# Turning and writing the gate weights of two pairs of images at once, in a MetaFormer block with a mixture of experts

## The chip, the cores and the metric

The kernel runs on one core of a Trainium2 chip. The metric is the device time of one execution in microseconds. The core has TensorE (PE, matmuls; PEld is its weight load), VectorE (DVE), ScalarE (ACT), GpSimd (POOL) and SyncE (SP), which here issues the transfers.

## What is computed

The input has 8 images of 64 channels and 16 x 16 pixels. After a layer norm over channels comes a convolutional linear attention, added to the input. The pixels are then tokens of 64 channels, and each passes a layer norm, a gate and eight experts:

```python
gate_logits = xf @ Wg + bg
top_w, top_i = jax.lax.top_k(gate_logits, TOP_K)          # TOP_K = 2
top_w = jax.nn.softmax(top_w, axis=-1)
w_dense = jnp.sum(jax.nn.one_hot(top_i, E, dtype=xf.dtype) * top_w[..., None], axis=1)
for e in range(E):                                        # E = 8
    h = jax.nn.gelu(xf @ W1[e] + b1[e], approximate=False)
    out = out + w_dense[:, e:e + 1] * (h @ W2[e] + b2[e])
x = from_tokens(t + out, x)
```

All is float32. `w_dense` (8 weights for each token, two of them not zero) is what the change is about.

## The kernel before

The eight images are worked on as four pairs, s = 0 to 3. A pair has 512 tokens: four tiles of 128, two for each image. All eight experts are computed for all tokens, and the result of each is multiplied by its gate weight.

**The gate.** VectorE works out the gate weights for two pairs together, a part (`softmax(0)` for pairs 0 and 1, `softmax(1)` for pairs 2 and 3). L808 writes them into `WDN`, where tokens lie on partitions. It runs at 66 us for part 0 and at 81 us for part 1.

**From there to where they are used.** An expert's result lies the other way, channels on partitions and tokens along the row. So the weights must be turned, and each row of them must stand on 64 partitions. This is done for each pair by itself: in `tokens(s)` TensorE makes two transposes of gate weights (L1079, one for each half of an image's tokens) into PSUM and then two transposes of the pair's tokens (L1082). In `read_tokens(s)` ScalarE copies the turned weights into `WT` (L509, 16 rows of 256) and the tokens into `outs`, which is `XP` in the profile (L510). SyncE, in `spread_weights(s)`, writes `WT` to memory (`spread_dram`, L308), waits for it to land, and then loads it back with every row repeated on 64 partitions into `WB` (L315; `WB` is part of `BAND` in the profile). `WB` has two slots, s % 2. From pair 2 on the loads also wait until the slot has been read.

**The experts.** `first_layer(s, e)` makes the hidden values of an expert (matmuls at L911, four of 512 columns), ScalarE applies gelu (L518), `second_layer(s, e)` (L1123) makes the result, recorded as eight matmuls of 256 columns. `combine(s, ep)` on VectorE takes two experts: `weigh` (L826) adds the bias and multiplies by `WB`, giving `WY`, and `add_up` (L832) adds it to `outs`. For the last pair GpSimd does seven of the eight additions (L396). `store(s)` (L322) writes a pair's result.

**The order** is written out by hand on each engine. On TensorE, around the change: `second_layer(0, 0..3)`, `tokens(0)`, `xt(3)` (four transposes, L1052), `first_layer(0, 7)`, `first_layer(1, 0..3)` with `gate(1)` in it, `second_layer(0, 4..7)`, `tokens(1)`, `first_layer(1, 4..7)`, `second_layer(1, 0..3)`, `tokens(2)`, `first_layer(2, 0..3)`, `second_layer(1, 4..7)`, `first_layer(2, 4..7)`, `second_layer(2, 0..3)`, `tokens(3)`, `first_layer(3, 0..3)`, `second_layer(2, 4..7)`, `first_layer(3, 4..7)`, `second_layer(3, 0..7)`. A result's place in PSUM is taken again once `y_read` says that VectorE has weighed what was there: `second_layer(0, 6)` waits for experts 0 and 1 of pair 0, `second_layer(1, 2)` for experts 4 and 5.

On SyncE, after the inputs: `spread_weights(0)`, `spread_weights(1)`, `store(0)`, `spread_weights(2)`, `store(1)`, `spread_weights(3)`, `store(2)`, `store(3)`.

Of the kernel before, what the change touches and what calls it, by code (L numbers as in the profile page):

```python
# [21 lines left out]
ALU = mybir.AluOpType  # L22
ACT = mybir.ActivationFunctionType
# [3 lines left out]
N = H * W  # L27
# [8 lines left out]
NW = HD + HEADS  # L36
E, HID, KC = 8, 256, 2
PAIRS = B // 2
TILES = 4
PT = TILES * 128  # L40
LN_C_EPS, LN_T_EPS, BN_EPS, ATT_EPS = 1e-6, 1e-5, 1e-5, 1e-15
# [28 lines left out]
def build(nc, x, w_qkv, w_dw, w_pw, w_proj, vectors, wg, w1, b1, w2, b2, consts, select, out):  # L70
    ctx = ExitStack()
    with ctx:  # L72
        def sb(name, shape, dt=F32):
            return ctx.enter_context(nc.sbuf_tensor(name, shape, dt))

        def sem(name):
            return ctx.enter_context(nc.semaphore(name))
# [4 lines left out]
        IDT = sb("IDT", [128, 128])  # L82
# [22 lines left out]
        SEL = sb("SEL", [LOW + DX * I, SELW], F32R)  # L105
        WD = sb("WD", [LOW + DX * I, G * DY], F32R)
        WGS = sb("WGS", [128, 2, E], F32R)
        WT = sb("WT", [2 * E, 2, N])
        W1H, W1L = sb("W1H", [128, E * HID], F32R), sb("W1L", [128, E * HID], F32R)
        RS = sb("RS", [128, G, DY, W])  # L110
        BAND = sb("BAND", [128, G * DY * 128])
# [11 lines left out]
        XBM = sb("XBM", [128, 16])  # L123
        SQ2 = sb("SQ2", [128, 2, TILES, C + 1])
        KR = sb("KR", [128, PAIRS, 4, HD])
        VM = sb("VM", [128, PAIRS, 2, 4, 2, KW])
        KV = sb("KV", [128, 2, 2, NW])
        DEN = sb("DEN", [128, 2, TILES, HEADS])
        SM = sb("SM", [128, PAIRS, 2, TILES])
        XS = sb("XS", [128, PAIRS, PT], F32R)  # L130
        PLACE = sb("PLACE", [128, 16, E], mybir.dt.uint32)
        GAP = sb("GAP", [128, 5, 16])
        WDN = sb("WDN", [128, PAIRS, 2, 2, E])

        band = BAND[:, :].rearrange("p (g d m) -> p g d m", g=G, d=DY)

# [4 lines left out]
        def late(*dims):  # L141
            first = taken[0]
            taken[0] += int(np.prod(dims))
            assert taken[0] <= G * DY * 128
            names = " ".join("abcde"[:len(dims)])
            return BAND[:, first:taken[0]].rearrange(f"p ({names}) -> p {names}", **dict(zip("abcde", dims)))
# [3 lines left out]
        QT = late(2, 2, N)  # L150
        ATT = late(2, TILES, HD)
        ATTT = late(2, PT)
        X2 = late(8, 2, C)
        XC2 = late(2, TILES, C)
        XHL = late(2, TILES, 2, C)
# [11 lines left out]

        outs = XP[:, :].rearrange("p (s n) -> p s n", s=PAIRS)

        PAR = CST[:, C_PAR:C_PAR + 2]  # L170

        PS = ctx.enter_context(nc.psum_tensor("PS", [128, 8, 512], F32))
        PARTS = 2
        OF_PART = PAIRS // PARTS
        SOFTMAX_PARTS = slice(0, OF_PART * TILES), slice(OF_PART * TILES, PAIRS * TILES)

        STATS_BANKS, WQC_BANK, WARM_BANK = (0, 1, 6, 2), 7, 7
# [11 lines left out]
        TOKEN_BANK = 5  # L189
# [35 lines left out]
        gap_ready, exp_ready, wdn_ready = sem("gap_ready"), sem("exp_ready"), sem("wdn_ready")  # L225
        turned, wt_read, tokens_read, wt_out = sem("turned"), sem("wt_read"), sem("tokens_read"), sem("wt_out")
# [55 lines left out]
        spread = nc.dram_tensor("spread_dram", (PAIRS, 2 * E, N), F32, kind="Internal").ap()  # L282
# [3 lines left out]
        @block.sync  # L286
        def _(sp):
            sp.dma_start(X[:, 0:2 * N], x[:, 0:2 * N]).then_inc(x_in[0], 16)
            sp.dma_start(X[:, 2 * N:4 * N], x[:, 2 * N:4 * N]).then_inc(x_in[1], 16)
            for h in range(2):  # L290
                sp.dma_start(WQ[C * h:C * h + C, :], w_qkv).then_inc(wq_in, 16)
            sp.dma_start(PW[:, :, :].rearrange("p g o -> p (g o)"),
                         w_pw.unsqueeze(0).broadcast_to([W, I, QKV])).then_inc(pw_in, 16)
            sp.dma_start(CST[:, :], consts).then_inc(cst_in, 16)
            sp.dma_start(VEC[:, :], vectors.unsqueeze(0).broadcast_to([128, 4 * C + E])).then_inc(vec_in, 16)
            sp.dma_start(WP[:, :], w_proj).then_inc(wp_in, 16)
            for h in range(2):
                sp.dma_start(WG[C * h:C * h + C, :], wg).then_inc(w1_in, 16)
                sp.dma_start(W1[C * h:C * h + C, :].rearrange("c (e n) -> c e n", e=E),
                             w1.rearrange("e c n -> c e n")).then_inc(w1_in, 16)  # L300
            sp.dma_start(W2[:, :, :].rearrange("p k c -> p (k c)"), w2).then_inc(w2_in, 16)
            sp.dma_start(B1[:, :], b1).then_inc(b1_in, 16)
            for h in range(2):
                sp.dma_start(B2[C * h:C * h + C, :], b2).then_inc(b2_in, 16)

            def spread_weights(s):
                sp.wait_ge(wt_read, s + 1)
                sp.dma_start(spread[s], WT[:, s % 2, :]).then_inc(wt_out, 16)  # L308
                sp.wait_ge(wt_out, 16 * (s + 1))
                if s >= 2:  # L310
                    sp.wait_ge(y_read, E * (s - 1))
                parts = ((0, 1), (1, 2), (2, 4)) if s == 0 else ((0, 2), (2, 4))
                for first, last in parts:
                    for b in range(2):
                        i = sp.dma_start(WB[C * b:C * b + C, s % 2, 2 * first:2 * last, :],  # L315
                                         spread[s, E * b + 2 * first:E * b + 2 * last, :].unsqueeze(0)
                                         .broadcast_to([C, 2 * (last - first), N]))
                        i.then_inc(wb_in[s % 2][first], 16)

            def store(s):  # L320
                sp.wait_ge(out_ready, s + 1)
                sp.dma_start(out[2 * s:2 * s + 2].rearrange("b c y x -> (b c) (y x)"), outs[:, s, :]).then_inc(stored, 16)  # L322

            spread_weights(0)
            spread_weights(1)
            store(0)
            spread_weights(2)
            store(1)
            spread_weights(3)
            store(2)  # L330
            store(3)
            sp.wait_ge(stored, 16 * PAIRS)
# [66 lines left out]
        def _(act):  # L399
# [104 lines left out]
            def read_tokens(s):  # L504

                act.wait_ge(turned, s + 1)
                if s >= 2:
                    act.wait_ge(wt_out, 16 * (s - 1))
                act.activation(WT[:, s % 2, :], PS[0:2 * E, TOKEN_BANK, N:2 * N], ACT.Copy).then_inc(wt_read, 1)  # L509
                act.activation(outs[:, s, :], PS[:, TOKEN_BANK, 0:N], ACT.Copy).then_inc(tokens_read, 1)  # L510

            def gelu(s, e):
# [56 lines left out]
        def _(dve):  # L569
# [223 lines left out]
            def softmax(part):  # L793
                tiles, pairs = SOFTMAX_PARTS[part], slice(OF_PART * part, OF_PART * (part + 1))
                O1, O2 = ONEHOT[:, 0, tiles], ONEHOT[:, 1, tiles]
                ex, dn, q1, q2 = (GAP[:, k, tiles] for k in (1, 2, 3, 4))

                def wide(v):
                    return v.unsqueeze(2).broadcast_to([128, tiles.stop - tiles.start, E])

                dve.wait_ge(exp_ready, part + 1)
                link(dve.tensor_scalar(dn, ex, 1.0, None, ALU.add))
                link(dve.reciprocal(q1, dn))
                link(dve.tensor_tensor(q2, ex, q1, ALU.mult))
                dve.tensor_tensor(O1, O1, wide(q1), ALU.mult)
                link(dve.tensor_tensor(O2, O2, wide(q2), ALU.mult))
                for b in range(2):
                    dve.tensor_tensor(WDN[:, pairs, :, b, :], O1.rearrange("p (s b h) e -> p b s h e", b=2, h=2)[:, b],  # L808
                                      O2.rearrange("p (s b h) e -> p b s h e", b=2, h=2)[:, b], ALU.add)\
                        .then_inc(wdn_ready, 1)  # L810

            def combine(s, ep):
# [96 lines left out]
        def _(pe):  # L909
# [146 lines left out]
            def gate(part):  # L1056

                pairs = range(OF_PART * part, OF_PART * (part + 1))
                for s in pairs:
# [11 lines left out]
            def tokens(s):  # L1071

                if s == 0:
                    pe.wait_ge(b_read[PAIRS - 1], B_PROJ)
                else:
                    pe.wait_ge(tokens_read, s)
                pe.wait_ge(wdn_ready, 2 * (s // OF_PART) + 2)
                for half in range(2):
                    pe.transpose(PS[0:2 * E, TOKEN_BANK, N + 128 * half:N + 128 * half + 128],  # L1079
                                 WDN[:, s, half].rearrange("p b e -> p (b e)"), IDT[:, :])  # L1080
                for half in range(2):
                    i = pe.transpose(PS[:, TOKEN_BANK, 128 * half:128 * half + 128],  # L1082
                                     X2[:, 2 * s + half].rearrange("p b c -> p (b c)"), IDT[:, :])
                i.then_inc(turned, 1)
# [147 lines left out]
```

## Time and profile before

| | |
|---|---|
| time, median of 3 runs | 127.3 us (127.17 to 127.38) |
| the profiled execution | 127.27 us, span 125.6 us |
| PE busy | 120.7 us (96%) |
| PEld busy | 98.1 us (78%) |
| VectorE busy | 85.9 us (68%) |
| ScalarE busy | 84.6 us (67%) |
| GpSimd busy | 28.7 us (23%) |
| granted TensorE clock | 1.000 |
| chain that ended last | PE 89%, DVE 3%, ACT 2% |

The span is from the first to the last instruction of the one execution that was profiled. The time has the start and the end of the execution besides. In rows of the trace, a line begins with the start in us from the beginning of the span and the time in us; "x16" is the number of instructions merged in the line, and what stands in brackets is the idle time of the engine before it and what ended it. Matmuls overlap, so several can be shown as running at the same time.

### The profile page before, as it was taken

What the parts mean: (1) busy time and instruction counts of PE and PEld (TensorE: products, weight loads), DVE (VectorE), ACT (ScalarE), POOL (GpSimd) and SP (SyncE); (2) the same over time, 40 slices, a digit from 0 to 9 for tenths busy, and PEclk for the clock granted to TensorE, in tenths of its full rate; (3) what the DMA queues carried; (4) which work ended last, traced back from release to release, by engine and by line L of the source; (5) the groups of instructions that cost most, each with busy time, mean ns of one, the idle gap of its engine ahead of it and who ended that gap; (6) DMA issues with size and microseconds to landing.
All of it is one profiled execution on the core that took longest, in us unless ns stands there. A gap on an engine that the chain in (4) does not pass through costs nothing.

```text
span 125.6 us, 2675 instructions
## 1 busy us (share of the span) xinstructions
PE 120.7 (96%) x916; PEld 98.1 (78%) x916; DVE 85.9 (68%) x273; ACT 84.6 (67%) x199; POOL 28.7 (23%) x35
## 2 busy tenths in 40 slices
PE   6999999999999999999999999999999999999990
PEld 6998899999999889897786786665866668666650
DVE  0789999999987887997985049991809155081552
ACT  4369999999973948159795597393782928739100
POOL 7007999600000000303280004000000000000681
PEclk9999999999999999999999999999999999999999
DMA  3789300000000000000000027039375100841001
GB/s 94 223 180 240 111 3 0 3 5 0 0 0 0 5 0 0 0 5 0 0 0 3 10 104 224 7 87 215 87 205 134 42 0 5 227 115 42 0 0 42
DMA packets 5078, 7.59 MB, mean 60 GB/s; under 512 B 1442, under 2 KB 3530, under 8 KB 5066
## 3 DMA queue, kind: packets, MB, share of 16 engines
q1 hardware_dynamic: 4832, 7.28, 22.0%
q10 hardware_dynamic: 234, 0.15, 0.4%
q8 instruction: 7, 0.11, 0.4%
q14 instruction: 5, 0.04, 0.1%
HBM read 6.84 MB, written 0.59 MB: 59 GB/s over the span
## 4 chain that ended last, share of the span: by engine, by line
PE 89%; DVE 3%; ACT 2%; issue 1%; POOL 1%; POOLq 1%; DVEq 0%
PE PS L911 57%; PE PS L1123 21%; PE PS L1015 3%; DVE MS L623 2%; PE PS L1021 2%; PE PS L927 1%; PE PS L1052 1%; POOL XP L396 1%; PE PS L1038 1%; PE PS L1079 1%; PE PS L975 1%; ACT RS L418 1%; PE PS L1082 1%; POOLq L72 1%; ACT MS L518 1%
## 5 line engine op out<-in xcount | busy, mean ns | idle before, releaser
L518 ACT ACTIVATE MS<-PS,B 128x512 f32<-128x512 f32 x48 | 28.9, 679 | 7.0 <-PE PS L911 7.0
L826 DVE SCALAR_TENSOR_TENSOR WY<-PS,B,BAND 128x256 f32<-128x256 f32 x32 | 14.4, 480 | 21.1 <-PE PS L1123 17.7
L911 PE MATMUL PS<-QP,BAND 128*128 128x120 f32 (+2 forms) x240 | 27.0, 275 | 0.2 <-DVE QP L646 0.2
L911 PEld LDWEIGHTS PS<-QP,BAND 128*128 128x128 f32 x240 | 26.9, 192 | 0.4 <-issue 0.4
L911 PE MATMUL PS<-XS,W1H 128*128 128x512 f32 x64 | 26.5, 414 | 0.0
L911 PE MATMUL PS<-XS,W1L 128*128 128x512 f32 x64 | 25.3, 396 | 0.0
L1123 PE MATMUL PS<-MS,W 128*64 128x256 f32 x192 | 22.3, 383 | 0.0
L1123 PEld LDWEIGHTS PS<-MS,W 128*64 128x64 f32 x192 | 13.2, 137 | 8.5 <-ACT MS L518 1.5
L436 ACT ACTIVATE BAND<-RS,PW 128x80 f32<-128x80 f32 x64 | 17.2, 429 | 0.0
L911 PEld LDWEIGHTS PS<-XS,W1H 128*128 128x128 f32 x64 | 12.0, 188 | 4.8 <-issue 0.9
L396 POOL TENSOR_TENSOR XP<-XP,WY 128x256 f32<-128x256 f32 x7 | 5.1, 727 | 41.1 <-DVE WY L826 40.2
L911 PEld LDWEIGHTS PS<-XS,W1L 128*128 128x128 f32 x64 | 12.1, 189 | 1.8
L376 POOL TENSOR_TENSOR SM<-SM,HALF 128x4 f32<-128x4 f32 x4 | 4.0, 1007 | 33.6 <-DVE SM L743 33.6
L832 DVE TENSOR_TENSOR XP<-XP,WY 128x256 f32<-128x256 f32 x25 | 10.5, 420 | 0.6 <-POOL XP L396 0.2
L579 DVE TENSOR_TENSOR BAND<-RS,PW 128x640 f32<-128x640 f32 x14 | 10.8, 807 | 0.0
L518 ACT ACTIVATE BAND<-PS,B 128x512 f32<-128x512 f32 x16 | 9.8, 698 | 0.0
L509 ACT ACTIVATE WT<-PS 16x256 f32<-16x256 f32 x4 | 1.5, 374 | 11.0 <-PE PS L1082 11.0
L1123 PE MATMUL PS<-BAND,W 128*64 128x256 f32 x64 | 7.6, 379 | 0.0
L1123 PEld LDWEIGHTS PS<-BAND,W 128*64 128x64 f32 x64 | 4.6, 137 | 2.3
L381 POOL TENSOR_TENSOR GAP<-EULER,GAP 128x8 f32<-128x8 f32 x2 | 3.3, 1636 | 12.0 <-DVE GAP L779 12.0
L649 DVE STREAM_TRANSPOSE QP<-MS 128x384 f32<-128x384 f32 x7 | 6.0, 858 | 0.0
L492 ACT ACTIVATE BAND<-PS 128x512 f32<-128x512 f32 x4 | 2.4, 597 | 4.9 <-PE PS L1038 4.9
(120 smaller groups left out, 168.6 us busy)
## 6 DMA issues: line engine op xcount, KB each, us to landing
BAND<-spread_dram SPq DMA_DIRECT2D x14, 256.0 KB, 4.6
W<-in_w_dram SPq DMA_DIRECT2D x3, 512.0 KB, 6.1
X<-in_x_dram SPq DMA_DIRECT2D x2, 256.0 KB, 3.2
BAND<-spread_dram SPq DMA_DIRECT2D x4, 128.0 KB, 2.9
out_dram<-XP SPq DMA_DIRECT2D x4, 128.0 KB, 1.7
VEC<-in_vectors_dram SPq DMA_DIRECT2D x1, 132.0 KB, 3.0
SELF<-in_select_dram ACTq DMA_DIRECT2D x1, 100.8 KB
WQ<-in_w_qkv_dram SPq DMA_DIRECT2D x2, 48.0 KB, 3.4
```

The source lines that it names most:

```text
L376: pool.tensor_tensor(SM[:, s, 1, :], SM[:, s, 0, :], HALF[:, 0:TILES], ALU.pow).then_inc(r2_ready, 1)
L381: pool.tensor_tensor(GAP[:, 1, tiles], EULER[:, tiles], GAP[:, 0, tiles], ALU.pow).then_inc(exp_ready, 1)
L396: pool.tensor_tensor(outs[:, s, :], outs[:, s, :], WY[:, e % 2, :], ALU.add).then_inc(added, 1)
L436: i = act.activation(band[:, g].rearrange("p d (x o) -> p o (d x)", o=I)[:, o], RS[:, g].rearrange("p d x -> p (d x)"), ACT.Copy, scale=PW ...
L518: act.activation(hidden(n), PS[:, h_bank(n), :], ACT.Gelu, bias=B1[:, k:k + 1]).then_inc(gelu_done, 1)
L579: dve.tensor_tensor(*band_factors(g), ALU.mult).then_inc(band_v, 1)
L649: dve.transpose(qp[:, 3 * h:3 * h + 3], head(h)).then_inc(qp_ready, 1)
L826: dve.scalar_tensor_tensor(out=WY[:, e % 2, :], in0=PS[:, bank, at:end], scalar=B2[:, e:e + 1], in1=WB[:, s % 2, e, :], op0=ALU.add, op1=A ...
L832: i = dve.tensor_tensor(outs[:, s, :], outs[:, s, :], WY[:, e % 2, :], ALU.add)
L911: return pe.matmul(PS[0:parts, bank, cols[0]:cols[1]], lhsT, rhs, start=start, stop=stop)
L1015: i = pe.matmul(PS[rows, CHAIN_BANK[s], 0:2 * KW], KR[:, s, r, rows], VM[:, s, half, r].rearrange("p b v -> p (b v)"), start=r == 0, stop= ...
L1123: i = pe.matmul(PS[C * b:C * b + C, bank, at:end], W2[:, KC * e + k, :], hidden(KC * (E * s + e) + k)[:, N * b:N * b + N], start=k == 0, s ...
```

## The change

The gate weights of a part, two pairs, are turned and written together. `WDN` is laid out anew, so that for one half of the tokens the 32 values of two pairs (2 pairs, 2 images, 8 experts) stand side by side. `tokens(s)` turns gate weights only for s = 0 and s = 2, with two transposes that give 32 rows, and waits for the gate only there. `read_tokens(s)` copies `WT` only there too, now 32 rows of 256. SyncE writes both pairs' weights in one transfer (`write_weights`), for part 0 ahead of `spread_weights(0)` and for part 1 ahead of `spread_weights(2)`. The loads themselves are as before, as are the transposes and copies of the tokens. The diff, but for the moved constants (`PARTS = 2`, `OF_PART = PAIRS // PARTS`):

```diff
@@ -105,7 +107,7 @@
         SEL = sb("SEL", [LOW + DX * I, SELW], F32R)
         WD = sb("WD", [LOW + DX * I, G * DY], F32R)
         WGS = sb("WGS", [128, 2, E], F32R)
-        WT = sb("WT", [2 * E, 2, N])
+        WT = sb("WT", [2 * OF_PART * E, PARTS, N])
         W1H, W1L = sb("W1H", [128, E * HID], F32R), sb("W1L", [128, E * HID], F32R)
         RS = sb("RS", [128, G, DY, W])
         BAND = sb("BAND", [128, G * DY * 128])
@@ -130,7 +132,7 @@
         XS = sb("XS", [128, PAIRS, PT], F32R)
         PLACE = sb("PLACE", [128, 16, E], mybir.dt.uint32)
         GAP = sb("GAP", [128, 5, 16])
-        WDN = sb("WDN", [128, PAIRS, 2, 2, E])
+        WDN = sb("WDN", [128, 2, PAIRS, 2, E])
 
         band = BAND[:, :].rearrange("p (g d m) -> p g d m", g=G, d=DY)
 
@@ -303,10 +303,13 @@
             for h in range(2):
                 sp.dma_start(B2[C * h:C * h + C, :], b2).then_inc(b2_in, 16)
 
+            def write_weights(part):
+                sp.wait_ge(wt_read, part + 1)
+                sp.dma_start(spread[OF_PART * part:OF_PART * (part + 1)].rearrange("s r n -> (s r) n"),
+                             WT[:, part, :]).then_inc(wt_out, 16)
+                sp.wait_ge(wt_out, 16 * (part + 1))
+
             def spread_weights(s):
-                sp.wait_ge(wt_read, s + 1)
-                sp.dma_start(spread[s], WT[:, s % 2, :]).then_inc(wt_out, 16)
-                sp.wait_ge(wt_out, 16 * (s + 1))
                 if s >= 2:
                     sp.wait_ge(y_read, E * (s - 1))
                 parts = ((0, 1), (1, 2), (2, 4)) if s == 0 else ((0, 2), (2, 4))
@@ -321,9 +324,11 @@
                 sp.wait_ge(out_ready, s + 1)
                 sp.dma_start(out[2 * s:2 * s + 2].rearrange("b c y x -> (b c) (y x)"), outs[:, s, :]).then_inc(stored, 16)
 
+            write_weights(0)
             spread_weights(0)
             spread_weights(1)
             store(0)
+            write_weights(1)
             spread_weights(2)
             store(1)
             spread_weights(3)
@@ -504,9 +509,9 @@
             def read_tokens(s):
 
                 act.wait_ge(turned, s + 1)
-                if s >= 2:
-                    act.wait_ge(wt_out, 16 * (s - 1))
-                act.activation(WT[:, s % 2, :], PS[0:2 * E, TOKEN_BANK, N:2 * N], ACT.Copy).then_inc(wt_read, 1)
+                if s % OF_PART == 0:
+                    act.activation(WT[:, s // OF_PART, :], PS[0:2 * OF_PART * E, TOKEN_BANK, N:2 * N], ACT.Copy)\
+                        .then_inc(wt_read, 1)
                 act.activation(outs[:, s, :], PS[:, TOKEN_BANK, 0:N], ACT.Copy).then_inc(tokens_read, 1)
 
             def gelu(s, e):
@@ -805,8 +810,8 @@
                 dve.tensor_tensor(O1, O1, wide(q1), ALU.mult)
                 link(dve.tensor_tensor(O2, O2, wide(q2), ALU.mult))
                 for b in range(2):
-                    dve.tensor_tensor(WDN[:, pairs, :, b, :], O1.rearrange("p (s b h) e -> p b s h e", b=2, h=2)[:, b],
-                                      O2.rearrange("p (s b h) e -> p b s h e", b=2, h=2)[:, b], ALU.add)\
+                    dve.tensor_tensor(WDN[:, :, pairs, b, :], O1.rearrange("p (s b h) e -> p b h s e", b=2, h=2)[:, b],
+                                      O2.rearrange("p (s b h) e -> p b h s e", b=2, h=2)[:, b], ALU.add)\
                         .then_inc(wdn_ready, 1)
 
             def combine(s, ep):
@@ -1074,10 +1079,11 @@
                     pe.wait_ge(b_read[PAIRS - 1], B_PROJ)
                 else:
                     pe.wait_ge(tokens_read, s)
-                pe.wait_ge(wdn_ready, 2 * (s // OF_PART) + 2)
-                for half in range(2):
-                    pe.transpose(PS[0:2 * E, TOKEN_BANK, N + 128 * half:N + 128 * half + 128],
-                                 WDN[:, s, half].rearrange("p b e -> p (b e)"), IDT[:, :])
+                if s % OF_PART == 0:
+                    pe.wait_ge(wdn_ready, 2 * (s // OF_PART) + 2)
+                    for half in range(2):
+                        pe.transpose(PS[0:2 * OF_PART * E, TOKEN_BANK, N + 128 * half:N + 128 * half + 128],
+                                     WDN[:, half, s:s + OF_PART].rearrange("p s b e -> p (s b e)"), IDT[:, :])
                 for half in range(2):
                     i = pe.transpose(PS[:, TOKEN_BANK, 128 * half:128 * half + 128],
                                      X2[:, 2 * s + half].rearrange("p b c -> p (b c)"), IDT[:, :])
```

## Rows read from the trace of the kernel before

**Rows 1.** One stretch: busy us of PE, PEld, DVE, ACT, POOL; PEclk, DMA share, GB/s.

```profile
41.00:119.00 78.00, 77.94 (x560) 57.61 (x556) 48.19 (x187) 51.83 (x99) 8.98 (x9) 1.00 0.23 61
```

**Rows 2.** The chain that ended last, in time: start, us, what.

```profile
76.47 3.60 PE PS L1123 x32
...
84.36 3.60 PE PS L1123 x32
87.96 0.32 PE PS L1079 x2
...
88.50 3.74 PE PS L911 x16
...
95.84 3.93 PE PS L911 x16
```

**Rows 3.** Timeline at `tokens(2)`: start, us, engine, line.

```profile
87.89 0.10 PEld L1079 LDWEIGHTS PS<-IDT,WDN 128*16 128x16 f32 x2 [0.39 <-issue]
87.89 0.39 PE L1079 MATMUL PS<-IDT,WDN 128*16 128x128 f32 x2
88.01 0.25 PEld L1082 LDWEIGHTS PS<-IDT,BAND 128*128 128x128 f32 x2
...
88.57 0.39 PE L911 MATMUL PS<-XS,W1L 128*128 128x512 f32 x1
```

**Rows 4.** Timeline, a changeover without `tokens`.

```profile
95.77 0.19 PEld L911 LDWEIGHTS PS<-XS,W1H 128*128 128x128 f32 x1 [0.38 <-issue]
...
96.11 0.40 PE L911 MATMUL PS<-XS,W1L 128*128 128x512 f32 x1
```

**Rows 5.** Timeline at `tokens(0)` and `xt(3)`, eight transposes.

```profile
69.86 0.39 PE L1079 MATMUL PS<-IDT,WDN 128*16 128x128 f32 x2
...
70.31 0.60 PE L1052 MATMUL PS<-IDT,BAND 128*128 128x128 f32 x4
...
70.98 0.39 PE L911 MATMUL PS<-XS,W1L 128*128 128x512 f32 x1
```

**Rows 6.** Groups of weight loads: busy us, mean ns, idle before.

```profile
L1082 PEld LDWEIGHTS PS<-IDT,BAND 128*128 128x128 f32 x8 | 1.0, 140 | 0.1
...
L1079 PEld LDWEIGHTS PS<-IDT,WDN 128*16 128x16 f32 x8 | 0.4, 89 | 1.5 <-issue 1.5
```

**Rows 7.** Timeline of ScalarE at `read_tokens(1)`.

```profile
80.65 0.37 ACT L509 ACTIVATE WT<-PS 16x256 f32<-16x256 f32 x1 [2.90 <-PE PS L1082]
80.93 0.36 ACT L510 ACTIVATE XP<-PS 128x256 f32<-128x256 f32 x1
```

**Rows 8.** Issues of transfers: count, KB each, median us to landing.

```profile
BAND<-spread_dram SPq DMA_DIRECT2D x14, 256.0 KB, 4.6
...
BAND<-spread_dram SPq DMA_DIRECT2D x4, 128.0 KB, 2.9
...
spread_dram<-WT SPq DMA_DIRECT2D x4, 16.0 KB, 1.4
```

**Rows 9.** Timeline of SyncE's queue: the time is that of the issues.

```profile
72.37 3.65 SPq L315 DMA_DIRECT2D BAND<-spread_dram  x6
...
82.47 2.37 SPq L315 DMA_DIRECT2D BAND<-spread_dram  x4
```

**Rows 10.** Timeline of VectorE's weighing, pairs 0 and 1.

```profile
76.57 0.88 DVE L826 SCALAR_TENSOR_TENSOR WY<-PS,B,BAND 128x256 f32<-128x256 f32 x2
...
81.22 0.87 DVE L826 SCALAR_TENSOR_TENSOR WY<-PS,B,BAND 128x256 f32<-128x256 f32 x2
...
87.38 0.88 DVE L826 SCALAR_TENSOR_TENSOR WY<-PS,B,BAND 128x256 f32<-128x256 f32 x2 [2.79 <-DMA BAND<-spread_dram]
```

**Rows 11.** Timeline of the tail.

```profile
117.00 5.95 POOL L396 TENSOR_TENSOR XP<-XP,WY 128x256 f32<-128x256 f32 x7 [40.24 <-DVE WY L826]
...
120.36 1.90 PE L1123 MATMUL PS<-BAND,W 128*64 128x256 f32 x16
...
122.31 0.48 DVE L826 SCALAR_TENSOR_TENSOR WY<-PS,B,BAND 128x256 f32<-128x256 f32 x1 [0.21 <-PE PS L1123]
```

More of the change, by code:

```diff
@@ L38 @@
 PAIRS = B // 2
+PARTS = 2
+OF_PART = PAIRS // PARTS
 TILES = 4
@@ L172, in build @@
         PS = ctx.enter_context(nc.psum_tensor("PS", [128, 8, 512], F32))
-        PARTS = 2
-        OF_PART = PAIRS // PARTS
         SOFTMAX_PARTS = slice(0, OF_PART * TILES), slice(OF_PART * TILES, PAIRS * TILES)
```

## The prediction

> **What bounds the kernel now.** I read the busy time by stretch first. From 41 to 119 us TensorE is busy for 77.94 of 78.00 us at a granted clock of 1.00, with ScalarE at 51.83 and VectorE at 48.19 [rows 1]. Both `tokens` steps that lose work lie in it. A step off TensorE can therefore gain nothing here unless TensorE waits for it, and a step on TensorE gains the time by which it keeps the next matmul back. But a busy figure is weak evidence, because matmuls overlap and their ends are modelled. So I read the chain of work that ended last, where TensorE's groups follow each other from `second_layer` through `tokens` to `first_layer` without a wait [rows 2], and then single starts, which are the firmest numbers that a trace has of a pipelined engine [rows 3 to 5]. What follows the last matmuls moves with them (the sum, below).
>
> **What the change removes on TensorE.** For pairs 1 and 3 the two transposes of gate weights go (L1079); the two transposes of tokens (L1082) stay. That is four transposes in all. Three readings of what one is worth lie far apart:
>
> - By duration a transpose takes 0.39 us for two overlapped ones [rows 3], over 0.7 us for the four if it added up. It doesn't: the next one starts long before.
> - By the chain the L1079 pair has 0.32 us [rows 2]. But all of `tokens` has 88.50 - 87.96 = 0.54 us there, and the sixteen matmuls behind it have less than where no `tokens` stands before them (3.93, at 95.84 [rows 2]); part of the 0.32 is the price of changing over from `second_layer`, which somebody pays in any case.
> - By starts: from the first weight load of `tokens` to the start of the second `first_layer` matmul it is 88.57 - 87.89 = 0.68 us [rows 3]. Without `tokens` the same distance is 96.11 - 95.77 = 0.34 us [rows 4]. So four transposes cost 0.34 us. With four more 128-column transposes between (`xt`, L1052) it is 70.98 - 69.86 = 1.12 us [rows 5], so one 128-column transpose costs (1.12 - 0.68)/4 = 0.11 us. If the two of L1082 take 0.22 of the 0.34, the two of L1079 take 0.12, which is 0.06 us each. The weight loads say the same directly: L1079's two start at 87.89 and L1082's first at 88.01 [rows 3], 0.12 us later.
>
> I take the last, because it is the one that says where L1082 would begin when L1079 is gone: at the changeover itself, its first load exposed just as the first load of `first_layer` is in rows 4. The gate transposes are cheap since their weight load has 16 columns and 89 ns, against 128 columns and 140 ns [rows 6]. Gain: 2 pairs x 0.12 = 0.24 us.
>
> **What it adds on TensorE.** The four transposes that remain in L1079 load 32 columns in place of 16. No row has 32. Between the two forms of rows 6 lie 51 ns for 112 columns, so 16 more are some 7 ns; the lower bound is nothing (the stream of 128 columns covers it), the upper the same 16 extra columns at the pace of a 128-column transpose (110 ns per 128, 14 ns). Four times: 0 to 0.06 us, I take 0.03, near the slope.
>
> A rule bears on this. The rows show 0.11 us from one 128-column transpose to the next and 0.06 us for a 16-column one. The Trainium skill, "TensorE: Matmul & The Clock Gate", section "Back-to-back issue gap", says that a stream of weight loads and matmuls is paced by both together and gives about 81 ns for 128 streamed columns; by that figure the four removed would give 0.32 us. No row here shows 81 ns. The same page's section "LDWEIGHTS (loading the stationary operand)" lets a weight load take its columns divided by 1.2, in ns: 107 for 128, with which the 0.11 us of the trace agree, and 13 for the 16 columns more, 0.05 us for four, within the bounds above.
>
> **ScalarE.** Two copies into `WT` go (L509). Its next copy starts 0.28 us after it [rows 7], so ScalarE gains 0.28 us per pair, twice what TensorE gains there, and its lead for the gelus behind `tokens` grows: no new wait. The remaining copies have 32 partitions in place of 16 and the same 256 elements in each; I cost them at nothing. VectorE's L808 writes the same 32 elements in another order; for pairs 2 and 3 it lies just ahead of the weighing at 81.22 [rows 10], over six microseconds before `tokens(2)` at 87.89, which covers any difference.
>
> **The queue of SyncE.** Pair 0: the one write is 32 KB in place of 16. 16 KB land in 1.4 us and 128 KB in 2.9 [rows 8], so 16 KB more are 0.2 us by that slope, and the loads of pair 0 leave 0.2 us late (the range is 0 to 1.4, the whole write once more). What hides it: the loads of experts 0 and 1 leave at 72.37 and some 0.6 us later, landing about 75.9 [rows 8, 9]; VectorE comes to them at 76.57 [rows 10]. TensorE wants those two results for expert 6, at 76.47 + 1.80 = 78.27 [rows 2], and VectorE has them by 77.45. Slack 0.7 + 0.8 = 1.5 us; cost nothing.
>
> Pair 1: no write, no wait for it. Its four loads (1 MB) leave at about 76.0, right behind pair 0's six [rows 9], not at 82.47. They meet pair 0's last loads, which leave from 75.4. Were those to land in twice their median 4.6 us [rows 8], they would be there at 84.6 and VectorE, which now takes expert 4 at 81.22 [rows 10], would be 3.4 us late; TensorE asks for that at 84.36 + 1.80 = 86.16 [rows 2], and 84.6 + 0.9 is before it. Covered still. In return VectorE's wait of 2.79 us for pair 1's load, up to 87.38 [rows 10], should all but vanish; what comes next is the last matmul of the second expert of pair 1, at 84.36 + 1.8 = 86.2. Nobody on TensorE waits for that work at that point, so it is worth nothing. The store of pair 0 and the second write stand behind this, as before. Pair 3's loads leave earlier too, right behind the store of pair 1, and are wanted only just before GpSimd's first addition at 117.00 [rows 11]. Nothing.
>
> **The sum.** The last matmuls begin at 120.36, VectorE's last weighing at 122.31, and GpSimd adds without a pause worth naming from 117.00 for 5.95 us [rows 11]: seven additions of 0.85 us against eight experts of 0.90 us on TensorE, so GpSimd follows TensorE and the tail moves as a whole. The profiled execution took 127.27 us with a span of 125.6, and the median of the three times is 127.3. 127.27 - 0.24 + 0.03 = 127.06, so 127.1. Its own range is 127.0 to 127.2. A difference of under 0.2%, 0.25 us, can't be told from none here.
>
> **The rivals.**
>
> 1. A removed transpose is worth a full pitch. The rows on starts fit a second reading: the two transposes of L1082 behind the changeover cost less than 0.11 each, and L1079 more. Then four at 0.11 are 0.44 us, 126.83; with the chain's 0.32 per pair as the far end, 126.63. For it speaks that the chain puts 0.32 on L1079, and that two starts inside a changeover are modelled; against it the weight loads, 0.12 apart. The 81 ns of the Trainium skill lie in between. Chance 0.2.
>
> 2. Slower: the doubled write keeps TensorE waiting in pair 0. Place: `second_layer(0, 6)`, which waits for `y_read` of experts 0 and 1, behind VectorE's first weighing. It decides from 1.5 us of delay of the loads. With the write slower by its own 1.4 us it would just miss; were 32 descriptors to take 2.0 us longer, 0.5 us come onto the path, and 127.56 results. Against it stand the 0.2 us of the slope and a queue that is otherwise empty there. Chance 0.07, with all other ways of losing over 0.25 us.
>
> 3. Nothing comes of it: the changeover after `second_layer`, where the weight loads stand idle for 0.39 us [rows 3], hides the short loads, and without them the 128-column load is merely exposed. 127.27, up to 127.3 with the wider loads. The rows with and without `tokens` both have this idle time (0.39 and 0.38 [rows 3, 4]), so the short loads don't lie inside it. Chance 0.15.
>
> **How the numbers follow.** The forecast has 0.58, of which a fifth falls over the edge of 0.25 us by its own spread. Faster by over 0.2%: 0.2 + 0.12 = 0.32. Slower by over 0.2%: 0.07. Within: 0.61. The range, 126.75 to 127.35, takes in the forecast, the third case and more than half of the first.
>
> **What would show it.** L1079 has four transposes, with 32 columns and some 95 ns per load, and L509 two copies. Behind `second_layer` in pairs 1 and 3, from the first load of L1082 to the start of the second `first_layer` matmul, 0.56 us (0.34 + 0.22); 0.45 or less would be rival 1, 0.68 rival 3. TensorE's last matmul, now from 120.36 [rows 11], and GpSimd's first addition, now at 117.00, are 0.2 us earlier. VectorE has no wait for a load of over 0.3 us. The first weighing of pair 0 is at 76.6 still; if it were past 78, rival 2. The prediction would be wrong altogether if TensorE shows a wait between 41 and 119 us that it doesn't have now, or if starts ahead of `tokens(0)` at 69.86 [rows 5], where nothing is changed, have moved by as much as the gain.

## The result, and the profile after

The changed kernel takes 127.18 us in the median (126.88 to 127.28), against 127.4 for the kernel before in runs beside it. The ratio, which is that of the means of 15 times each, is 0.9976, with a 95% interval of 0.9967 to 0.9985: 0.31 us less, between 0.19 and 0.42. (The medians alone differ by 0.22 us.) The forecast was 127.1 us, a difference of 0.21.

The page of the profile after, its first lines (line numbers have moved down by 3 to 6, so L315 is now L318, L911 L916, L1079 L1085, L1082 L1088, L1123 L1129, L509 L513, L826 L831):

```profile
span 125.2 us, 2658 instructions
...
PE 119.5 (95%) x912; PEld 96.8 (77%) x912; DVE 85.9 (69%) x273; ACT 84.4 (67%) x197; POOL 28.7 (23%) x35
```

Its issues of transfers:

```profile
spread_dram<-WT SPq DMA_DIRECT2D x2, 32.0 KB, 1.5
```

TensorE has four instructions fewer (912 against 916) and ScalarE two (197 against 199). The write of 32 KB lands in 1.5 us where 16 KB took 1.4 [rows 8]. The busy time of one stretch answers to [rows 1]: TensorE has as little idle time as before.

```profile
41.00:119.00 78.00, 77.94 (x560) 57.59 (x558) 48.58 (x187) 51.68 (x97) 9.31 (x9) 1.00 0.23 61
```

The chain that ended last, in time, answers to [rows 2]:

```profile
76.51 3.60 PE PS L1129 x32
80.11 0.37 PE PS L1088 x2
80.48 3.72 PE PS L916 x16
84.21 3.60 PE PS L1129 x32
87.81 0.33 PE PS L1085 x2
88.14 0.22 PE PS L1088 x2
88.36 3.74 PE PS L916 x16
```

Before, `second_layer(0, 4..7)` began at 76.47 and `first_layer` of pair 2 at 88.50 [rows 2], 12.03 us later. Now they are 88.36 - 76.51 = 11.85 us apart. 0.18 us went at `tokens(1)`.

Starts are finer. The timeline at `tokens(1)`, where L1085 is no more:

```profile
80.04 0.20 PEld L1088 LDWEIGHTS PS<-IDT,BAND 128*128 128x128 f32 x2 [0.39 <-issue]
80.05 0.44 PE L1088 MATMUL PS<-IDT,BAND 128*128 128x128 f32 x2
80.21 0.19 PEld L916 LDWEIGHTS PS<-XS,W1H 128*128 128x128 f32 x1
80.24 0.48 PE L916 MATMUL PS<-XS,W1H 128*128 128x512 f32 x1
80.32 0.19 PEld L916 LDWEIGHTS PS<-XS,W1L 128*128 128x128 f32 x1
80.56 0.39 PE L916 MATMUL PS<-XS,W1L 128*128 128x512 f32 x1
```

I call the distance from the first weight load of a `tokens` step to the start of the second matmul of the `first_layer` behind it the step's **distance**. Here it is 80.56 - 80.04 = 0.52 us, against 0.68 with the gate transposes [rows 3], 0.56 forecast. The gain is 0.16 us for a pair.

A second measure is the stretch from the first weight load of `tokens(0)` to the start of VectorE's last addition, since nothing ahead of it is changed and the start of it wanders by up to 0.5 us from profile to profile. I call it the **back part**. Before, it is 122.98 - 69.86 = 53.12 us:

```profile
122.98 0.42 DVE L832 TENSOR_TENSOR XP<-XP,WY 128x256 f32<-128x256 f32 x1 [0.18 <-POOL XP L396]
```

After:

```profile
69.89 0.11 PEld L1085 LDWEIGHTS PS<-IDT,WDN 128*32 128x32 f32 x2 [0.38 <-issue]
...
116.67 5.96 POOL L401 TENSOR_TENSOR XP<-XP,WY 128x256 f32<-128x256 f32 x7 [39.87 <-DVE WY L831]
...
122.66 0.42 DVE L837 TENSOR_TENSOR XP<-XP,WY 128x256 f32<-128x256 f32 x1 [0.19 <-POOL XP L401]
```

122.66 - 69.89 = 52.77 us, 0.35 less, about twice what `tokens(1)` brought (0.03 us between the two measures are not accounted for). GpSimd's additions moved from 117.00 [rows 11] to 116.67 as a whole.

VectorE and SyncE changed as forecast. VectorE waits for no load any more, and what it waits for at pair 1 is the second expert's matmul; the first weighing of pair 0 has stayed where it was in [rows 10]:

```profile
76.61 0.88 DVE L831 SCALAR_TENSOR_TENSOR WY<-PS,B,BAND 128x256 f32<-128x256 f32 x2
...
86.24 0.88 DVE L831 SCALAR_TENSOR_TENSOR WY<-PS,B,BAND 128x256 f32<-128x256 f32 x2 [1.61 <-PE PS L1129]
```

```profile
72.45 6.21 SPq L318 DMA_DIRECT2D BAND<-spread_dram  x10
```

### The profile page after: what moved, and what is told of

Read it like the earlier page. It is cut to its first block, busy times and chain, and to the rows that moved or that the text cites. A ratio compares the mean times of both kernels' runs of the same rounds, so it can differ in the third digit from the quotient of the medians.

```text
span 125.2 us, 2658 instructions
## 1 busy us (share of the span) xinstructions
PE 119.5 (95%) x912; PEld 96.8 (77%) x912; DVE 85.9 (69%) x273; ACT 84.4 (67%) x197; POOL 28.7 (23%) x35
## 4 chain that ended last, share of the span: by engine, by line
PE 82%; DVE 5%; ACT 3%; DMA 2%; POOL 2%; issue 2%; POOLq 1%; DVEq 0%
PE PS L916 53%; PE PS L1129 19%; PE PS L1020 3%; DMA X<-in_x_dram 2%; POOL XP L401 2%; DVE STATS L595 2%; ACT MS L418 2%; PE PS L1026 2%; PE PS L1057 1%; DVE XP L589 1%; PE PS L1043 1%; PE PS L1088 1%; PE PS L980 1%; POOLq L74 1%; PE PS L1085 1%
## 5 line engine op out<-in xcount | busy, mean ns | idle before, releaser
L831 DVE SCALAR_TENSOR_TENSOR WY<-PS,B,BAND 128x256 f32<-128x256 f32 x32 | 14.4, 481 | 20.7 <-PE PS L1129 20.0
L916 PE MATMUL PS<-QP,BAND 128*128 128x120 f32 (+2 forms) x240 | 27.0, 275 | 0.2 <-DVE QP L651 0.2
L916 PEld LDWEIGHTS PS<-QP,BAND 128*128 128x128 f32 x240 | 26.9, 192 | 0.4 <-issue 0.4
L916 PE MATMUL PS<-XS,W1H 128*128 128x512 f32 x64 | 26.5, 414 | 0.0
L916 PE MATMUL PS<-XS,W1L 128*128 128x512 f32 x64 | 25.3, 396 | 0.0
L1129 PE MATMUL PS<-MS,W 128*64 128x256 f32 x192 | 22.3, 383 | 0.0
L1129 PEld LDWEIGHTS PS<-MS,W 128*64 128x64 f32 x192 | 13.2, 137 | 8.5 <-ACT MS L523 1.5
L916 PEld LDWEIGHTS PS<-XS,W1H 128*128 128x128 f32 x64 | 12.0, 188 | 4.7 <-issue 0.9
L916 PEld LDWEIGHTS PS<-XS,W1L 128*128 128x128 f32 x64 | 12.1, 189 | 1.8
L1129 PE MATMUL PS<-BAND,W 128*64 128x256 f32 x64 | 7.6, 379 | 0.0
L1129 PEld LDWEIGHTS PS<-BAND,W 128*64 128x64 f32 x64 | 4.6, 137 | 2.3
L373 POOL TENSOR_TENSOR INV<-INV,HALF 128x32 f32<-128x32 f32 x1 | 5.5, 5463 | 0.1
```

Of the source, the lines that this page charges most:

```text
L373: pool.tensor_tensor(INV[:, 1, 0:C // 2], INV[:, 0, 0:C // 2], HALF[:, 0:C // 2], ALU.pow).then_inc(inv_ready, 1)
L831: dve.scalar_tensor_tensor(out=WY[:, e % 2, :], in0=PS[:, bank, at:end], scalar=B2[:, e:e + 1], in1=WB[:, s % 2, e, :], op0=ALU.add, op1=A ...
L916: return pe.matmul(PS[0:parts, bank, cols[0]:cols[1]], lhsT, rhs, start=start, stop=stop)
L1129: i = pe.matmul(PS[C * b:C * b + C, bank, at:end], W2[:, KC * e + k, :], hidden(KC * (E * s + e) + k)[:, N * b:N * b + N], start=k == 0, s ...
```

## The experiments

Two questions: is all of the gain TensorE's, and what does a transpose cost? Every transpose here streams 128 columns. Theory A says that it costs 0.107 us for them, whatever its weight load has, and that only the first one behind a changeover has its load exposed. Theory B gives a part of the gain to ScalarE or the loads. Theory C is the prediction's step: a transpose costs by the columns of its weight load, 0.06 us for 16. All kernels are the changed one with an edit; ratios are to the kernel before.

**two_16: the gate transposes alone put back.**

```diff
+                else:
+                    for m in range(2):
+                        pe.transpose(PS[0:2 * E, TOKEN_BANK, N + 128 * (m % 2):N + 128 * (m % 2) + 128],
+                                     WDN[:, m % 2, s].rearrange("p b e -> p (b e)"), IDT[:, :])
```

> The changed kernel, with the two 16-column gate transposes put back into `tokens(1)` and `tokens(3)` and nothing else of the old form (their output is not used; copies, write and loads stay as changed). Theory A, TensorE alone: all of the gain (0.31 us by the ratio 0.9976) comes from these four transposes; the distance from the first weight load of `tokens(1)` to the second `first_layer` matmul goes back from 0.52 to 0.68 us, and the time back to that of before, ratio 0.999 to 1.001. Theory B, that the saved copies on ScalarE or the earlier loads bring a part of it: the distance is 0.68 us too, but the ratio stays at 0.9990 or below.

```profile
80.04 0.10 PEld L1089 LDWEIGHTS PS<-IDT,WDN 128*16 128x16 f32 x2 [0.39 <-issue]
...
80.72 0.39 PE L916 MATMUL PS<-XS,W1L 128*128 128x512 f32 x1
```

Measured: distance 80.72 - 80.04 = 0.68 us, back part 123.01 - 69.88 = 53.13 us, as before the change to 0.01. Ratio 0.9992 (0.9983 to 1.0001), which left a tenth of a microsecond open. So it was run again, with three others beside it:

> two_16 once more. The first time its interval, 0.9983 to 1.0001, held both theories. Theory A, TensorE alone: ratio 1.000, within 0.0005. Theory B, a part of the gain is elsewhere: 0.9990 or below a second time, and clearly below 1.

Measured: 0.9997 (0.9988 to 1.0007), back part 122.93 - 69.80 = 53.13. Theory A holds in the time too. Theory B asked for 0.9990 or below; what the interval still allows it is about 0.15 us, and the back part, alike to 0.01 us in three profiles, nothing.

**after_again: the changed kernel once more, beside the same runs of the kernel before.**

> The changed kernel itself once more, beside the next three, so that all four stand against the same runs of the kernel before. Ratio 0.997 to 0.998; from the first start of `tokens(0)` to VectorE's last addition 52.8 us, against 53.1 in the kernel before.

Measured: 0.9962 (0.9949 to 0.9975), back part 122.89 - 70.11 = 52.78 us. The ratio lies below the expected 0.997 to 0.998. The two intervals of the changed kernel overlap from 0.9967 to 0.9975; a gain of 0.32 to 0.42 us suits both. The trace's 0.35 is in it.

**six_16: six gate transposes.** The edit is that of two_16 with `range(6)`.

> As two_16, but with six 16-column gate transposes in `tokens(1)` and `tokens(3)` (outputs not used). Theory A, stream: every transpose costs 0.107 us for its 128 streamed columns, however few columns its weight load has, and only the first one behind the changeover has its load exposed; distance 0.68 + 4 x 0.107 = 1.11 us, time 0.86 us above before (ratio 1.0067). Theory C, columns (the prediction's step): a 16-column transpose costs 0.06 us; distance 0.68 + 0.24 = 0.92 us, time 0.48 us above before (1.0038).

Measured: 1.0062 (1.0047 to 1.0077), back part 124.00 - 69.98 = 54.02 us. Its timeline at `tokens(1)`:

```profile
80.14 0.54 PEld L1089 LDWEIGHTS PS<-IDT,WDN 128*16 128x16 f32 x6 [0.39 <-issue]
80.14 0.82 PE L1089 MATMUL PS<-IDT,WDN 128*16 128x128 f32 x6
80.69 0.25 PEld L1092 LDWEIGHTS PS<-IDT,BAND 128*128 128x128 f32 x2
...
81.25 0.40 PE L916 MATMUL PS<-XS,W1L 128*128 128x512 f32 x1
```

The distance is 81.25 - 80.14 = 1.11 us, as Theory A has it; four more transposes of 16 columns cost 0.43 us, 0.107 each. Theory C's 0.92 us falls, and its 1.0038 lies outside the interval. The six loads take 0.54 us and one of them 0.09, so the sixth begins 0.45 us after the first. With the first step at next to nothing (0.01, below) the other four are 0.11 each.

**two_128: two wide transposes in the same place.**

```diff
+                else:
+                    for half in range(2):
+                        pe.transpose(PS[:, TOKEN_BANK, N + 128 * half:N + 128 * half + 128],
+                                     X2[:, 2 * s + half].rearrange("p b c -> p (b c)"), IDT[:, :])
```

> As two_16, but the two transposes put into `tokens(1)` and `tokens(3)` have 128 columns (the tokens turned a second time, output not used). Theory A, stream: distance at `tokens(1)` 0.52 + 2 x 0.107 = 0.73 us, that is 0.05 us more than with two of 16 columns, all of it the exposed first load. Theory C, columns: 0.68 + 2 x 0.05 = 0.78 us.

Measured: distance 80.79 - 80.06 = 0.73 us, which is Theory A's number and not Theory C's 0.78; back part 123.13 - 69.90 = 53.23. One time, 127.39 us. Against two_16, 0.05 us more at each of the two places: eight times the columns, and only the first load shows.

**tokens_first: wide loads first in `tokens(0)` and `tokens(2)`.** The two loops of `tokens(s)` change places, and the semaphore is raised by the last transpose.

> The changed kernel with the order of transposes turned round in `tokens(0)` and `tokens(2)`: the two of the tokens (128 columns) first, the two of the gate weights (32 columns) behind them. Theory A, stream, with the first load behind a changeover exposed by its columns: the exposed load has 128 columns in place of 32, and the distance from the first load to the second `first_layer` matmul grows from 0.68 to 0.72 us. Theory C, a transpose costs by its columns wherever it stands: the same four loads, 0.68 us. The time can't tell them apart (0.08 us in all).

Measured: distance at `tokens(2)` 88.41 - 87.68 = 0.73 us against 0.68, back part 122.64 - 69.76 = 52.88 against 52.77. The same transposes in another order cost 0.05 us more each time: what is exposed is the first load. Theory C expected 0.68 us. The one time, 126.90 us, can't tell the two apart.

```profile
87.68 0.20 PEld L1083 LDWEIGHTS PS<-IDT,BAND 128*128 128x128 f32 x2 [0.39 <-issue]
...
87.85 0.21 PEld L1088 LDWEIGHTS PS<-IDT,WDN 128*32 128x32 f32 x2
...
88.41 0.40 PE L916 MATMUL PS<-XS,W1L 128*128 128x512 f32 x1
```

**loads_late: the loads held back.**

```diff
             spread_weights(0)
+            sp.wait_ge(tokens_read, 2)
             spread_weights(1)
...
             store(1)
+            sp.wait_ge(tokens_read, 4)
             spread_weights(3)
```

> The changed kernel, with SyncE held before the loads of pair 1 until `tokens(1)` is read and before those of pair 3 until `tokens(3)` is read, so that they leave at about 81 and 104 us, as in the kernel before less the write. Theory A, TensorE alone: the loads' earlier leave was worth nothing, ratio 0.9976 as the changed kernel; VectorE's first weighing of pair 1 may be where it is in the changed kernel (86.2) or 0.2 us behind. Theory B, that the earlier loads bring a part: at least 0.1 us lost, 0.9984 or above.

Measured: 0.9969 (0.9957 to 0.9981), back part 122.70 - 69.91 = 52.79 us. The loads of pair 3 left at 104.08 in place of 97.94, and nothing changed. Both edits together:

> two_16 with SyncE held as in loads_late: of the change, the one wider write, the two saved copies and the two saved writes are left. Theory A: ratio 1.000, as two_16_again. Theory B with the loads as the cause: 1.000 where two_16_again is below; with the copies or writes as the cause: as far below 1 as two_16_again.

Measured: 1.0009 (0.9987 to 1.0031), back part 123.06 - 69.93 = 53.13 us. What is left of the change there, the wider write and the saved copies and writes, moves nothing in the back part; the interval of the times, 0.28 us to either side, is too wide to say so by itself.

**write_x2 and write_x3: the loads of pair 0 late, to price the rival on the slow side.** The edit, here for two:

```diff
-                sp.dma_start(spread[...], WT[:, part, :]).then_inc(wt_out, 16)
-                sp.wait_ge(wt_out, 16 * (part + 1))
+                for m in range(2):
+                    sp.dma_start(spread[...], WT[:, part, :]).then_inc(wt_out, 16)
+                    sp.wait_ge(wt_out, 16 * (2 * part + m + 1))
```

> The changed kernel with the write of the turned gate weights made twice, one behind the other and both waited for, so the loads of pair 0 leave 1.5 us later. By the slack read in the prediction (0.7 us until VectorE comes to them and 0.8 us until TensorE asks for the result) nothing is lost: ratio 0.9976, with VectorE's first weighing at 77.3 to 77.6 in place of 76.6. Were the slack smaller, each missing 0.1 us would cost 0.1 us.

Measured: 1.0026 (1.0011 to 1.0042), with times from 127.34 to 128.13 us. The expectation of no loss was wrong. Its chain:

```profile
76.63 1.04 PE PS L1130 x7
77.67 0.04 issue
77.72 0.89 DVE WY L832 x2
78.60 0.14 issue
78.74 1.95 PE PS L1130 x16
80.69 0.37 PE PS L1089 x2
```

The loads left at 74.03, 4.02 us after the first load of `tokens(0)`, where it is 72.45 - 69.89 = 2.56 in the changed kernel: 1.46 later. VectorE's first weighing began at 77.72 in place of 76.61, and TensorE went on at 78.74, 0.14 us after it ended. How late that is, starts tell. The changed kernel:

```profile
76.44 1.95 PE L1129 MATMUL PS<-MS,W 128*64 128x256 f32 x16
78.22 1.90 PE L1129 MATMUL PS<-BAND,W 128*64 128x256 f32 x16
80.05 0.44 PE L1088 MATMUL PS<-IDT,BAND 128*128 128x128 f32 x2
```

write_x2:

```profile
78.74 1.95 PE L1130 MATMUL PS<-BAND,W 128*64 128x256 f32 x16 [0.23 <-DVE WY L832]
80.62 0.44 PE L1089 MATMUL PS<-IDT,BAND 128*128 128x128 f32 x2
```

Expert 6 begins 1.78 us after expert 4 in the changed kernel (78.22 - 76.44). In write_x2 expert 4 begins at 76.56, so the place of expert 6 was 78.34, and it began 0.40 us late. From there to `tokens(1)` it is 80.62 - 78.74 = 1.88 us in place of 80.05 - 78.22 = 1.83, 0.05 more. The back part is 123.25 - 70.01 = 53.24 us, 0.47 more, and 0.40 + 0.05 come to about that. So 1.46 - 0.47 = 1.0 us was covered. The chain's 1.95 us for these matmuls, against 1.80 in a chain without a stop, must not be read as a stop that costs 0.15: behind a stop the chain counts from the first start, else it runs some 0.07 us behind the starts (76.51 against 76.44).

> As write_x2 with the write three times, the loads of pair 0 some 3.0 us later. By the slack of 1.5 us, 1.5 us come onto TensorE's path at expert 6 of pair 0 (a wait of TensorE on VectorE's L831): 128.6 us, ratio 1.009. If VectorE's later softmax of part 1 delays `tokens(2)` nothing more is added, since that has 6 us. A rival: TensorE never waits, since the slack is larger than read, and the ratio stays below 1.000.

Measured: 1.0173 (1.0107 to 1.0239), back part 124.77 - 70.08 = 54.69 us, 1.92 more in place of 1.5. One of the four times, 130.69 us, raises the ratio; the other three, 129.02 to 129.14, lie near 1.013. TensorE waits for VectorE, which waits for the load. The waits of this kernel (us in total, times, longest):

```profile
DVE WY L832 <- DMA BAND<-spread_dram: 2.8, 2, 2.5
...
PE PS L1130 <- DVE WY L832: 1.7, 1, 1.7
```

Its loads left at 75.58, 5.50 us after `tokens(0)` began, 1.48 later than in write_x2, and the back part is 1.45 us longer: from there on the kernel loses what the loads lose. The place is the one that the prediction named; the slack is 5.50 - 2.56 - 1.92 = 1.0 us again, not 1.5.

**one_64: one gate transpose for both halves.**

```diff
-        WT = sb("WT", [2 * OF_PART * E, PARTS, N])
+        WT = sb("WT", [4 * OF_PART * E, PARTS, 128])
-        WDN = sb("WDN", [128, 2, PAIRS, 2, E])
+        WDN = sb("WDN", [128, PARTS, 2, OF_PART, 2, E])
...
-                sp.dma_start(spread[OF_PART * part:OF_PART * (part + 1)].rearrange("s r n -> (s r) n"),
+                sp.dma_start(spread[OF_PART * part:OF_PART * (part + 1)].rearrange("s r (h n) -> h (s r) n", h=2),
...
-                    for half in range(2):
-                        pe.transpose(PS[0:2 * OF_PART * E, TOKEN_BANK, N + 128 * half:N + 128 * half + 128],
-                                     WDN[:, half, s:s + OF_PART].rearrange("p s b e -> p (s b e)"), IDT[:, :])
+                    pe.transpose(PS[0:4 * OF_PART * E, TOKEN_BANK, N:N + 128],
+                                 WDN[:, s // OF_PART].rearrange("p h s b e -> p (h s b e)"), IDT[:, :])
```

> The changed kernel with one gate transpose in place of two for a part: the weights of both halves of the tokens stand side by side (64 columns), the turned ones take 64 rows of 128, ScalarE's copy is 64 x 128, and the write orders them in memory as before. Theory A, stream: `tokens(0)` and `tokens(2)` lose 0.107 us each and pay 0.01 to 0.02 for the longer exposed load; distance at `tokens(2)` 0.68 - 0.09 = 0.59 us, time 0.18 us below the changed kernel, ratio to before 0.9962. Theory C, columns: 64 columns cost what two times 32 do; distance 0.67 to 0.68 us, no gain over the changed kernel (0.9976).

Measured: distance at `tokens(2)` 88.58 - 87.99 = 0.59 us, as Theory A has it; back part 122.82 - 70.22 = 52.60 us, 0.17 less than the changed kernel. Ratio 0.9962 (0.9949 to 0.9976), whose interval overlaps that of the changed kernel. In the timeline of SyncE the loads of pair 0 leave 2.46 us after the write is issued, not 1.51, and VectorE waits for them:

```profile
71.08 0.61 SPq L308 DMA_DIRECT2D spread_dram<-WT  x1
73.54 6.24 SPq L318 DMA_DIRECT2D BAND<-spread_dram  x10
```

```profile
77.30 0.88 DVE L831 SCALAR_TENSOR_TENSOR WY<-PS,B,BAND 128x256 f32<-128x256 f32 x2 [0.49 <-DMA BAND<-spread_dram]
```

> one_64 once more, beside the changed kernel in the same call. Its trace says 0.17 us less than the changed kernel between `tokens(0)` and the end, so a ratio to before 0.0013 below that of after_again. If the slower landing of its write (2.46 us until the loads leave, against 1.51) reaches TensorE in some runs, it is no better than after_again.

Measured: 0.9958 (0.9946 to 0.9970), 0.0004 below after_again and not 0.0013. In this profile VectorE waits 0.85 us for the first load, up to 77.50, and TensorE's expert 6 stands at 78.52 where 76.51 + 1.78 = 78.29 was its place; back part 122.94 - 70.06 = 52.88 us. The 0.95 us by which the loads leave later take up nearly all of the 1.0 us of slack, and the rest hangs on the landing: VectorE began 3.76 us after the loads left in one_64 (77.30 - 73.54) and 4.14 us in one_64_again (77.50 - 73.36). So in one of the two profiles the slower write takes back what the transposes give, and the back part of this kernel differs by 0.28 us between them. Whether one_64 beats the changed kernel is open; beside the changed kernel itself it was lower by 0.0004, well inside both intervals. Why its write is slower (twice the rows, each half as long) was not taken apart.

## Why the prediction was right, and where its sum was off

*What bounds the kernel.* Right. The whole gain is on TensorE: two_16 puts it back with four transposes alone, to 0.01 us in the back part and to about 0.15 us in the times. loads_late shows that the earlier loads don't matter, and the back part of two_16_late that the rest doesn't.

*What the four transposes are worth.* The sign and the place are right, the term is too small: 0.24 us forecast, 2 x 0.16 = 0.32 by the distances, 0.35 by the back part and 0.36 (2 x 0.18) by the chain. The step that failed is where L1082 would begin "its first load exposed just as the first load of `first_layer` is in rows 4". That first load holds the next one back by 0.11 us. But it is another kind of load: 188 ns in `first_layer`, 140 ns in a transpose, both with 128 columns. Groups of weight loads in the profile after:

```profile
L916 PEld LDWEIGHTS PS<-XS,W1H 128*128 128x128 f32 x64 | 12.0, 188 | 4.7 <-issue 0.9
...
L1088 PEld LDWEIGHTS PS<-IDT,BAND 128*128 128x128 f32 x8 | 0.9, 140 | 0.8 <-issue 0.8
...
L1085 PEld LDWEIGHTS PS<-IDT,WDN 128*32 128x32 f32 x4 | 0.2, 96 | 0.8 <-issue 0.8
```

At the changeover the two loads of L1088 take 0.20 us together (80.04), so the second begins 0.20 - 0.14 = 0.06 us after the first, and the next one 0.11 us after that, at 80.21. The L1079 pair of [rows 3] reads anew in the same way: 0.10 us for two loads of 89 ns, so the second begins 0.01 us after the first, and then 0.11 us pass to the load of L1082. Its 0.12 us were never two times 0.06 but 0.01 + 0.11. Taking the pair away saves two full steps of 0.107 and exposes a wider first load, 0.06 in place of 0.01: 0.214 - 0.05 = 0.16 us. The reason that the prediction gave for cheap gate transposes, the 16 columns of their loads, falls with it: in six_16 they cost as much as wide ones. six_16, two_128, one_64 and tokens_first each hit a distance worked out so, to 0.01 us.

So the rival of the full pitch was half right: each transpose is worth 0.107, but the one at the changeover is partly covered. Its 0.44 us didn't come, nor the 0.64 of the chain.

*Where the 0.107 us come from* is not shown. Weight loads of 16 and of 128 columns give the same step, so the load doesn't set it. That the 128 streamed columns do is an inference, since no run has a transpose with fewer. Nor is it a floor under every step: in the profile after, the matmuls of L1020 (loads of 64 columns, 130 streamed) are recorded as sixteen in 1.11 us at 0.27 for one, (1.11 - 0.27)/15 = 0.06 us apart; but the program has eight matmuls for the sixteen records, and a transpose has one record.

*The 32 columns.* 0.03 us forecast for four. The distance at `tokens(2)` is 88.42 - 87.74 = 0.68 us as before, so it is under 0.01 for two. Right in size, since a load is exposed only once: by tokens_first 96 columns more are 0.05 us, and 16 would be under 0.01. The rule of the Trainium skill named there, of the page "TensorE: Matmul & The Clock Gate", section "LDWEIGHTS (loading the stationary operand)", gives 107 ns for 128 columns. The trace agrees for the loads of `first_layer` (in the kernel before the first starts at 95.77 and the second at 95.88), not for those of the transposes, where the first holds back the second by 0.06 us: there the measurement decides. The Trainium skill's 81 ns for 128 streamed columns, in the section "Back-to-back issue gap", is the step of no transpose here; six_16 has 107. That four times 81 ns is 0.32 us, the gain by the distances, is a coincidence, since the 0.32 are four steps of 107 less two times 0.05.

*ScalarE.* Nothing, as costed. At `tokens(1)` it starts its copy of the tokens at 80.52 where the copy of `WT` had been at 80.65 [rows 7].

*The queue.* The extra landing time was 0.1 us (0.2 forecast), VectorE's wait of 2.79 us [rows 10] is gone and worth nothing, and what came next was what the prediction named, at 86.24 (86.2 forecast). The slack of pair 0's loads was read as 1.5 us and is 1.0. Small terms were left out. VectorE began 3.66 us after the first issue in write_x3 (79.24 - 75.58) where the prediction had 75.9 - 72.37 = 3.5. TensorE went on 0.14 us after VectorE's result. By starts it asks for the results 1.78 us behind 76.40, at 78.18, not at 78.27. A stop costs it 0.05 us more than the wait. The rival on the slow side had the right place and mechanism, but it begins at 1.0 us.

*The sum.* 127.27 - 0.24 + 0.03 should have read 127.27 - 0.32 + 0.01 = 126.96, and the profiled execution took 126.93. That the median, 127.18, lies 0.12 above the forecast although the gain was larger comes from the base: the kernel before had 127.4 in these runs, not 127.27. The difference came out just over the line of 0.2% that the text had set, 0.24% in place of 0.17%. So the outcome was the one to which the prediction gave 0.32, and not the likeliest, with 0.61; but the interval, 0.15% to 0.33%, has the line inside it. Only after_again, with 0.25% to 0.51%, lies wholly beyond.

## What to carry to other kernels

On an engine that never waits, an instruction is worth its step to the next start, not its duration and not its share of the chain; take steps from starts, and split a merged group's time by the duration of one (0.10 us for two of 0.09 means that they began together). A transpose whose weight load has few columns is not a cheap one: here it took the same step as a wide one, so put two small ones into one load (0.09 us at each place in one_64). Before making a chain of transfers longer, add up what the waiting engine has in hand, with half a microsecond for landings that scatter (3.66 to 4.14 us here).

## What the runs showed of the hardware

- Steps between back-to-back transposes were 0.107 us for 128 streamed columns, with loads of 16 as of 128 columns. The duration of a transpose's weight load was 89, 96, 108 and 140 ns for 16, 32, 64 and 128 columns, and that of a matmul of `first_layer` 188 ns for 128.
- Behind a stop of TensorE in the middle of `second_layer`, sixteen matmuls took 1.88 us from their first start to the next group's, in write_x2, write_x3 and one_64_again, and 1.83 without a stop.
- A write of 32 KB as 64 rows of 512 bytes held its follower back 2.46 us (one_64), as 32 rows of 1 KB 1.51 us (the changed kernel).
- Profiles differ by up to 0.5 us ahead of all that was edited: the first weight load of `tokens(0)` stood between 69.76 and 70.22 us, and the first matmul of the convolution between 13.39 and 13.87, in step with it. The back part of one kernel agreed to 0.01 us in the repeats of the changed kernel and of two_16, but not in those of one_64 (52.60 and 52.88), where a load came late. For a change of 0.3 us on TensorE one back part said more than the times did.
